# Four graph attention layers on one core: the attention weights of heads 2 and 3 of the multi-head layer transposed by the DMA crossbar in 16-bit halves

## What is computed

```python
# layer 0: scores from two weight matrices, softmax over neighbours
h1, h2, h3 = h @ W1, h @ W2, h @ W3
e = where(adj > 0, leaky_relu(h1 @ h2.T, 0.2), -1e12)
out0 = relu(softmax(e) @ h3)
# layers 1 and 3: 4 heads, scores are the sum of a row and a column term
e = where(adj > 0, leaky_relu(e_src[:, None] + e_dst[None, :], 0.2), -9e15)
out1 = elu(concat_heads(softmax(e) @ Wh))
# layer 2: multi-head attention, 4 heads of 64, biases, output projection, layernorm
s = where(adj == 0, -inf, (Q @ K.T) / 8)
out2 = layernorm(concat_heads(softmax(s) @ V) @ Wo + bo) * gamma + beta
```

## Time and profile before

| | |
|---|---|
| median of 3 runs | 2945.29 us (2944.38 to 2945.89) |
| profiled execution: span | 2943.7 us |
| around the span | not recorded apart; the median stands 1.6 us above the span |
| busy share PE / DVE / ACT / POOL | 98% / 72% / 57% / 28% |
| mean granted clock of TensorE | 0.997 of full speed |

### The profile page before, as it was taken

How to read it: one execution, slowest core, us unless ns; L and a number is a source line. 1 busy time by engine, 2 the same in 40 slices (tenths; PEclk the granted TensorE clock), 3 DMA queues, 4 the chain that set the end, 5 groups by cost and what they waited for, 6 DMA issues and landing times.

```text
span 2943.7 us, 68275 instructions
## 1 busy us (share of the span) xinstructions
PE 2887.3 (98%) x27732; PEld 2034.8 (69%) x27732; DVE 2127.5 (72%) x5596; ACT 1682.3 (57%) x3554; POOL 827.8 (28%) x917
## 2 busy tenths in 40 slices
PE   7899999999999999999999999999999999999998
PEld 5566767666767666767667767667767667776766
DVE  5576787776787776877776877776877777877764
ACT  2555655655656655656655656656656656656543
POOL 2123222323222323222233232233222233222221
PEclk9999999999999999999999999999999999999999
DMA  3001011101011101011101011101011111011010
GB/s 102 22 23 45 27 41 45 44 23 45 23 44 45 44 23 44 23 44 44 38 30 44 23 45 44 37 30 44 23 45 44 34 33 40 28 37 37 17 36 30
DMA packets 58840, 109.89 MB, mean 37 GB/s; under 512 B 5568, under 2 KB 41408, under 8 KB 58528
## 3 DMA queue, kind: packets, MB, share of 16 engines
q1 hardware_dynamic: 58032, 104.61, 10.8%
q0 software_dynamic: 496, 0.92, 0.3%
HBM read 88.21 MB, written 17.30 MB: 36 GB/s over the span
## 4 chain that ended last, share of the span: by engine, by line
PE 77%; DVE 12%; POOL 6%; issue 2%; ACT 1%; SPq 0%; DMA 0%; POOLq 0%; DVEq 0%; ACTq 0%
PE ps L972 19%; PE ps L1080 11%; PE ps L1106 8%; PE ps L1115 8%; PE ps L978 8%; PE ps L1142 8%; PE ps L1029 8%; PE ps L958 4%; DVE stats L641 3%; POOL rstd L367 3%; POOL xc L417 3%; DVE pB L753 2%; PE ps L1017 2%; DVE nb L658 1%; DVE hn L829 1%
## 5 line engine op out<-in xcount | busy, mean ns | idle before, releaser
L389 POOL TENSOR_TENSOR qx<-qx,xc 128x512 f32<-128x512 f32 x128 | 163.7, 1279 | 869.4 <-ACT qx L529 869.4
L641 DVE BATCH_NORM_STATS2 stats<-xc 128x6 f32<-128x256 f32 x384 | 134.7, 413 | 328.6 <-POOL xc L399 264.1
L448 ACT ACTIVATE hn<-xc,nb,rstd 128x256 f32<-128x256 f32 x384 | 209.1, 592 | 163.9 <-DVE nb L658 160.7
L1080 PEld LDWEIGHTS ps<-vals,pA 128*64 128x64 f32 x8192 | 253.9, 138 | 54.6 <-issue 54.5
L972 PE MATMUL ps<-wgat,hT 128*128 128x264 f32 x1024 | 267.4, 395 | 1.8 <-ACT hT L457 1.8
L1080 PE MATMUL ps<-vals,pA 128*64 128x65 f32 x8192 | 266.4, 223 | 2.1 <-DVE pA L753 2.0
L1080 PE MATMUL ps<-vals,pB 128*64 128x65 f32 x8192 | 264.0, 223 | 0.3 <-DVE pB L753 0.2
L1080 PEld LDWEIGHTS ps<-vals,pB 128*64 128x64 f32 x8192 | 249.7, 138 | 16.8 <-issue 16.7
L457 ACT COPY hT<-ps 128x1024 f32<-128x1024 f32 x128 | 129.7, 1013 | 224.0 <-PE ps L958 219.8
L1106 PE MATMUL ps<-qx,qT 64*128 64x512 f32 x1024 | 249.8, 614 | 1.1 <-DVE hn L767 0.8
L364 POOL TENSOR_SCALAR rstd<-mv 128x4 f32<-128x4 f32 x160 | 75.0, 469 | 610.2 <-DVE mv L650 610.2
(11 more groups left out here) (147 smaller groups left out, 6194.3 us busy)
## 6 DMA issues: line engine op xcount, KB each, us to landing
qT<-r_dram SPq DMA_DIRECT2D x64, 512.0 KB, 3.9
hT<-r_dram SPq DMA_DIRECT2D x64, 512.0 KB, 4.9
x_in<-in_x SPq DMA_DIRECT2D x32, 512.0 KB, 3.9
out_x<-xc SPq DMA_DIRECT2D x32, 512.0 KB, 3.0
pX<-in_adj SPq DMA_DIRECT2D x1, 1024.0 KB, 8.1
r_dram<-growT SPq DMA_DIRECT2D x64, 8.0 KB, 1.3
pX<-in_L_gnn_W SPq DMA_DIRECT2D x2, 256.0 KB, 5.2
pA<-in_L_gnn_a POOLq DMA_DIRECT2D x8, 64.0 KB, 8.8
```

Of the source, the lines that this page charges most:

```text
L641: last = nc.vector.bn_stats(stats[s][:, t, :], src[:, t, :])
L1080: last = nc.tensor.matmul(ps[lo:hi, BANK[f"G{g}.{h}"], t * DV:(t + 1) * DV], gat_p[s][h % 2][:, j, t * P + lo:t * P + hi], vals[s][:, j, h ...
```

## The change

**Transposes.** The weights of heads 0 and 1 are transposed as before. Those of heads 2 and 3 (8 of 16 tiles of a sample) no longer go through PE. Each such tile takes three steps. A split copies the 128 x 512 float32 tile, seen as 128 x 1024 16-bit words, to a buffer `halves`, with all even words first and all odd words behind them. SP issues one `dma_start_transpose`, which transposes the 128 x 1024 words in blocks of 128 and writes them back over the tile's own place in `prob2`. A join interleaves even and odd words again into `probT2`. There are three buffers `halves` (`RING` = 3), used in the order of `TURNS`; a split waits until the transpose three turns earlier has landed.

```diff
+        halves = [sb(f"halves{r}", [P, 2, N], u16) for r in range(RING)]
...
+        TURNS = (
+            (2, (2, 2, 0)), (2, (2, 3, 0)), (2, (2, 2, 1)), (2, (2, 3, 1)), (2, (2, 3, 2)),
+            (2, (2, 3, 3)), (2, (2, 2, 3)), (1, (2, 2, 2)),
+        )
...
+            def landed(self, eng, w, tile, before=0):
+                if w is None:
+                    return
+                i = self.at[w.c, tile]
+                if i // RING + 1 - before > 0:
+                    eng.wait_ge(self.sems[i % RING], 16 * (i // RING + 1 - before))
...
+        def turn(sp, w, tile):
+            sp.dma_start_transpose(words(w, tile).rearrange("p (b n) -> p b n", n=P),
+                                   turns.half(w, tile)[:, :, :].rearrange("p q n -> p (q n)")).then_inc(
+                                       turns.sem_of(w, tile), 16)
...
+            def split2(w, h, t):
+                if w is None:
+                    return
+                p2_ready[h].wait(act, w, t + 1)
+                turns.landed(act, w, (2, h, t), 1)
+                nc.scalar.copy(turns.half(w, (2, h, t))[:, :, :], pairs(w, (2, h, t))).then_inc(split_by_act.sem, 1)
...
+            def join2(w, h, t):
+                if w is None:
+                    return
+                turns.landed(dve, w, (2, h, t))
+                nc.vector.tensor_copy(joined(w, (2, h, t)), flat(w, (2, h, t))).then_inc(pT2_dve[h].sem, 1)
```

**SP's list** is now one with the other engines' and carries the transposes:

```diff
+            def slot(z, a, b, c, d, e):
+                spread(b, 1); turn2(c, 2, 0); turn2(c, 3, 0); turn2(c, 2, 1); turn2(c, 3, 1); turn2(c, 3, 2)
+                load_next(b); turn2(c, 3, 3); turn2(c, 2, 3); store(d); spread(c, 3); turn2(b, 2, 2)
```

**Order.** The slot has a sample more in its arguments (z is n+1, e is n-4) and there are 34 slots. The end of layer 3 of a sample is now done in the slot after. The first layernorm of z is taken one slot early. PE's list begins with the last transposes of heads 0 and 1, the last two `gat_aggregate` of d and `aggregate2(c, 0)`. The second pair of heads comes later than before:

```diff
-                aggregate2(c, 0)
-                gnorm[3].wait(pe, d, 4); weights_transposed2(c, 3, 0); weights_transposed2(c, 2, 2)
-                weights_transposed2(c, 2, 3); weights_transposed2(c, 3, 1); weights_transposed2(c, 3, 2)
-                pT2_act[2].wait(pe, c, 2); weights_transposed2(c, 3, 3); inverse_spread(c, 0)
-                pT2_dve[2].wait(pe, c, 2); inverse_spread(c, 1); aggregate2(c, 1); gat_aggregate(b, 1, 0)
...
+                weights_transposed2(c, 1, 1); inverse_spread(c, 0); rT_out[1].wait(pe, b)
+                weights_transposed2(c, 1, 2); gnorm[3].wait(pe, d, 2); weights_transposed2(c, 0, 2)
+                pT2_act[0].wait(pe, c, 2); weights_transposed2(c, 1, 3); weights_transposed2(c, 0, 3)
...
+                gat_aggregate(d, 3, 2)
...
+                pT2_act[1].wait(pe, c); gat_aggregate(d, 3, 3); pT2_dve[0].wait(pe, c, 2); pT2_act[1].wait(pe, c, 2)
+                aggregate2(c, 0); transposed(a, 0, 0); transposed(a, 0, 1); transposed(a, 0, 2); transposed(a, 0, 3)
+                gat_aggregate(b, 1, 0); u_columns(a, 0); u_columns(a, 1)
...
+                gnorm[1].wait(pe, b); gat_aggregate(b, 1, 1)
...
+                gat_aggregate(b, 1, 2); scores0(a, 0)
...
+                inverse_spread(c, 1)
...
+                gat_aggregate(b, 1, 3)
...
+                pT2_dve[2].wait(pe, c); pT2_act[3].wait(pe, c); aggregate2(c, 1); scores0(a, 1)
+                oT_ready.wait(pe, c, 2); scores0(a, 2); scores0(a, 3); masked0.wait(pe, a, 2); o_rows(c, 0)
+                o_rows(c, 1); o_rows(c, 2); o_rows(c, 3); masked0.wait(pe, a, 3); v_rows(a, 0, 0); v_rows(a, 0, 1)
```

DVE's list up to that point, and ACT's up to its last split:

```diff
+                gat_norm(d, 3, 1); gat_weights(d, 3, 3, 0, 1, 2); weights_out2(c, 1, 1); gat_weights(d, 3, 3, 3)
+                pT2p_ready[0].wait(dve, c, 3); weights_out2(c, 1, 2); weights_out2(c, 0, 2); weights_out2(c, 0, 3)
+                gat_norm(d, 3, 2); gat_norm(d, 3, 3); gat_weights(b, 1, 0, 0, 1, 2, 3)
+                gat_weights(b, 1, 1, 0, 1, 2, 3); gat_weights(b, 1, 2, 0); gat_norm(b, 1, 0); gat_out(d, 3, 0)
+                gat_weights(b, 1, 2, 1); inverse_sums2(c, 1); gat_weights(b, 1, 2, 2); agg2_ready.wait(dve, c)
+                join2(c, 3, 1); gat_weights(b, 1, 2, 3); gat_out(d, 3, 1); gat_norm(b, 1, 1)
+                gat_weights(b, 1, 3, 0, 1, 2, 3); join2(c, 3, 2); join2(c, 3, 0); join2(c, 2, 3); gat_norm(b, 1, 2)
...
+                weights_out2(c, 0, 1); gat_exp(b, 1); exp2(c, 2, 3); elu_relu(d, 3, 0); exp2(c, 3, 1)
+                elu_min(d, 3, 0); pT2p_ready[0].wait(act, c, 4); weights_out2(c, 1, 3); exp2(c, 3, 2)
+                elu_exp(d, 3, 0); weights_out2(c, 1, 0); split2(c, 3, 1); elu_relu(d, 3, 1); elu_min(d, 3, 1)
+                elu_m[3].wait(act, d, 2); normalised(a, 0, 0); normalised(a, 0, 1); normalised(a, 0, 2)
+                normalised(a, 0, 3); h_transposed(a, 0); exp2(c, 3, 3); inverse_out(c, 0); elu_exp(d, 3, 1)
+                split2(c, 3, 2); split2(c, 3, 3); split2(c, 2, 3); join2(c, 2, 1); xg_ready[3].wait(act, d, 2)
+                u_out(a); join2(c, 2, 0); inverse_columns(c, 1); join2(c, 2, 2); agg2_ready.wait(act, c)
```

More of the change, by code:

```diff
@@ L60, in sets @@
             return [sb(f"{name}{s}", shape) for s in range(SETS)]
-        x_in = sets("x_in", [P, NT, C])
+        x_in = [sb(f"x_in{s}", [P, NT, C]) for s in range(X_SETS)]
         xc = sets("xc", [P, NT, C])
@@ L256, in gnn_stack_kernel, with in_order @@
         x2_ready = Signal("x2_ready")
+        TURNS = (
+            (2, (2, 2, 0)), (2, (2, 3, 0)), (2, (2, 2, 1)), (2, (2, 3, 1)), (2, (2, 3, 2)),
+            (2, (2, 3, 3)), (2, (2, 2, 3)), (1, (2, 2, 2)),
+        )
+        SPLIT_BY_POOL = (
+            (2, (2, 2, 1)), (1, (2, 2, 2)), (1, (2, 2, 0)), (1, (2, 3, 0)),
+        )
+        SPLIT_BY_ACT = (
+            (2, (2, 3, 1)), (2, (2, 3, 2)), (2, (2, 3, 3)), (2, (2, 2, 3)),
+        )
+        def in_order(plan, first):
+            steps = list(first)
+            steps += [(n - stage, tile) for n in range(1, B + LAST) for stage, tile in plan
+                      if 0 <= n - stage < B]
+            return {step: i for i, step in enumerate(steps)}
@@ L284, in rows_in, with slots @@
             return ps[:, bank:bank + 2, :].rearrange("p b (t c) -> p (b t) c", c=C)
[L286 to L290, removed]
+        def slots(first, slot):
+            first(Work(0), Work(1))
+            for n in range(1, B + LAST):
+                slot(*[Work(n - d) if 0 <= n - d < B else None for d in range(-1, 5)])
         block = ctx.enter_context(nc.Block())
@@ L296, in _, with load @@
         def _(sp):
[L297 to L301, removed]
+            def load(w, ahead=X_SETS):
+                sp.dma_start(x_in[w.x][:, :, :], x_dram[w.c + ahead]).then_inc(x_loaded[w.x], 16)
             def store(w):
@@ L326, in spread, with turn2, first @@
                     sp.dma_start(dst[:, :, :], src.broadcast_to([P, 2, N])).then_inc(r_loaded[g].sem, 16)
[L328 to L331, removed]
+            def turn2(w, h, t):
+                if w is None:
+                    return
+                line = next(n for n in (split_by_act, split_by_pool) if (w.c, (2, h, t)) in n.at)
+                line.wait(sp, w, (2, h, t))
+                turn(sp, w, (2, h, t))
+            def slot(z, a, b, c, d, e):
+                spread(b, 1); turn2(c, 2, 0); turn2(c, 3, 0); turn2(c, 2, 1); turn2(c, 3, 1); turn2(c, 3, 2)
+                load_next(b); turn2(c, 3, 3); turn2(c, 2, 3); store(d); spread(c, 3); turn2(b, 2, 2)
+            def first(a, z):
+                pass
             load(Work(0), 0)
@@ L341, in _ @@
                 sp.sem_inc(x_stored[s], 16)
-                if s > 0:
+                if 0 < s < X_SETS:
                     load(Work(s), 0)
-            for n in range(B + 2):
-                slot(*[Work(n - d) if 0 <= n - d < B else None for d in range(SETS)], more=n + SETS < B)
+            slots(first, slot)
             for s in range(SETS):
@@ L621, in first @@
+                q_out(a, 1, 1); gat_row_exp(a, 1)
                 act.wait_ge(bias_in, BIASES)
                 act.wait_ge(setup_ok, SETUP)
-            slots(act, first, slot)
+            slots(first, slot)
         @block.vector
@@ L1218, in slot @@
[L1218 to L1222 removed]
+                    idle_turns(3, 5)
+                gat_aggregate(b, 1, 2); scores0(a, 0)
+                if b is None and c is not None:
+                    idle_turns(3, 32)
+                inverse_spread(c, 1)
+                if a is None and b is not None:
+                    idle_turns(3, 5)
@@ new lines, in slot @@
+                aggregate0(a, 3); qk_columns(b, "KT", 0); qk_columns(b, "QT", 1)
+                if a is None and b is not None:
+                    idle_turns(5, 10)
+                if b is None and c is not None:
+                    idle_turns(1, 76)
+                transposed(c, 3, 0); transposed(c, 3, 1); transposed(c, 3, 2); transposed(c, 3, 3)
+                qk_columns(b, "KT", 1)
+                if b is None and c is not None:
+                    idle_turns(1, 4)
+                q_rows(c, 3, 0); q_rows(c, 3, 1); qT_ready.wait(pe, b, 2); q_rows(c, 3, 2); q_rows(c, 3, 3)
@@ L1281, in first @@
                 pe.wait_ge(setup_ok, SETUP)
-            slots(pe, first, slot)
```

(1 more changed line is left out.)

344 lines of the change are left out of this document (166 added, 178 removed), and 15 rows, old and new, of the table BANK.

## The result

The changed kernel takes 2981.16 us, median of 4 runs (2973.41 to 2995.30), against 2944.84 before: 1.0126 times as long, 95% interval 1.0096 to 1.0157. It is slower by 1.3%. Faster, at 2864 us, was forecast. The four runs lie 22 us apart, and the profiled one (2973.41) is the shortest of them.

The account below looks back on a forecast made before the run. PE was taken to bound the steady slots: 30 x (3.55 won - 0.7 stall) = 85.5 us off 2943.7, plus 4 for the ends and 1.6 from span to median, gave 2864 us; range 2826 to 2950.

Parts of the forecast that it names:

- The bound and PE's gain: Steady slots: PE sets the time, and losing 32 transposes of heads 2 and 3 saves 3.55 us a slot.
- The 0.7 us of stall in the sum: Before `aggregate2(c, 1)`: PE waits for DVE's joins, offered at 25.5 us but asked at 24.9; about 0.7 us a slot.
- a sign of being wrong: Start of layer 1: the forecast is wrong if `gat_weights(b, 1, 0)` waits for `r_dram` in every slot.
- The step that failed: ACT in a steady slot: four copies out, four splits and four joins in; +5.7 us, to 58 of 85, hidden.
- the ends: First and last slots: idle turns added, transposes removed; together +4 us, between -5 and +15.
- The crossbar: SP's eight transposes a slot: 256 KB lands in about 2.6 us, step 1.3 to 2; up to 2.3 costs nothing.
- The place I feared: The seven turns before `aggregate2(c, 1)`: the kernel is slower from a crossbar step of about 2.8 us a tile.
- My rival on the slower side: Seven turns before `aggregate2(c, 1)`: at 4 us a tile, a stall of 12 us a slot, 3205 us; chance 0.17.
- Rival 1: DVE's early part: slow joins, broadcasts behind a transpose, or uncovered layer-2 chain; 2 to 3.3 us a slot; chance 0.16.
- DVE's early part: First part of a slot: DVE's tiles and joins are offered within a microsecond of when PE asks for them.
- The chain of layer 2's end: Layer 2's end: 17.9 us covered by 18.5 of PE work, charged at nothing; up to 2 us a slot if uncovered.
- the third rival: Slow crossbar step; as an extra, PE's idling may drop its clock from 2.4 to 1.2 GHz; chance 0.17.

## Why the prediction was wrong

**The bound and PE's gain: right.** 3.55 us a slot was forecast for the transposes; 3.63 came back for 3.65 of work put in again. That four buffers reach 85.84, where 85.75 was forecast, is in part luck. The 0.7 us of stall in the sum stood before `aggregate2(c, 1)`, for DVE's joins; no wait of PE for a join is in the list of four buffers. It waits about as long elsewhere, 0.7 us a slot before the first product of layer 1, for `gat_weights(b, 1, 0)`, which waits for `r_dram`. The prediction had named that very wait as a sign of being wrong.

**The step that failed** is "ACT gives up four copies ... and gets four splits and four joins ...: +5.7, to 58 of 85, hidden". I added up ACT's busy time and left out the wait that each split brings with it, `turns.landed(act, w, ..., 1)`, and so never asked what is queued behind it. ACT's busy time is indeed 58.45 in the slot. But (3,1) is three turns behind (2,0), (2,0) stands behind the broadcasts on SP, and the layernorm of a, on which PE waits next, stands behind (3,1). I had drawn up that very queue on SP, and used it only for the product at its far end, `aggregate2(c, 1)`. The place where the ring makes an engine wait was never priced. ACT waited 3.9 us a slot there and PE 2.0 for ACT; with what follows on PE, the transposes fed tile by tile and the products at the lower clock, the slot became 3.2 us longer than without the wait, where 0.7 had been allowed for all stalls. Taking the wait away alone, by a fourth buffer or by the order of ACT's list, gave 100 and 92 us back.

**The arithmetic of the miss.** Mean slot 89.0 instead of 85.75, over 29 to 30 slots: some 95 us. The rest is in the ends. From the first `scores0` product of sample 2 to that of sample 31 the four-buffer kernel needs 29 slots; what lies outside is 390.7 us, and 374.0 before. So the ends cost 17 us and not 4, the second term that was mis-sized. In the last slot with layer 2 in it PE has 39 idle turns between the two pairs of heads, about 9 us, in the kernel of four buffers, where 24 transposes took 2.7 in the same slot before. That is some 6 of the 17 us; where the rest went is open:

```profile
2810.22 7.41 PE L1065 MATMUL ps<-ident 128*128 128x128 f32 x64
2817.47 0.60 PE L1224 MATMUL ps<-ident,qx 128*128 128x128 f32 x4
2817.91 1.73 PE L1065 MATMUL ps<-ident 128*128 128x128 f32 x14
```

**The crossbar.** I took 2.6 us to landing and a step of 1.3 to 2. The shortest landing was 3.0, the median 4.3, and a turn holds SP for 1.27 (median). The place I feared, the wait for the last join, is nearly free. Of the two figures of the Trainium skill, that of "Advanced Engine Details and Errata", section "X-Bar Transpose (TRN2)", agrees with the runs in the medians, 4.3 us against 4.7 for a plain copy; the shortest were 3.0 and 2.2. That of "VectorE: DVE Perf Modes", section "The three transpose paths", taken block by block, does not hold for eight blocks in one DMA: an estimated 10.5 us by it, and none took over 8.0 with broadcasts in front. My rival on the slower side had the right sign and the right queue, SP's, but the wrong place and mechanism; its 3205 us are far off. Rival 1 had about the right size, 2 to 3.3 us of stall a slot, and none of its three causes was the one.

**DVE.** A join takes 0.75 us and not 1.1, on ACT 1.36 and not 1.01; POOL's splits are at 1.36. DVE's early part was offered within a microsecond of what PE wants, as forecast: with four buffers PE waits 0.7 us a slot for it. The chain of layer 2's end stayed covered: no wait of PE in that part stands in the list with more than a few entries.

**The clock.** Named in the third rival as an extra, not priced. It came, but in 15 of 28 slots and at an estimated 22 us of the 91. A forecast with such a gap has to count more than the gap: here the mean slot grew by 3.2 us for 2.0 us of wait.

## What to carry to other kernels

When an edit gives an engine work that begins with a wait, look at what that engine does next and for whom: price the wait at that place, not the engine's share. A ring of buffers that is filled faster than a DMA lands puts its wait into the engine that fills it, and one more buffer, or one instruction moved behind the urgent ones, is worth nearly as much here (92 to 100 us) as all the work that was saved (113 us when it was put in again). Ask of every DMA not only how long it takes but what is in front of it in its queue, and compare the order of the queue with the order in which its landings are needed.

## What the runs showed of the hardware

A crossbar transpose of 128 x 1024 16-bit words from SBUF to SBUF lands in 4.3 us (median of 256) where a plain DMA copy of the same size in its place takes 4.7. The shortest landings are 3.0 and 2.2 us, and one issue holds SP for 1.27 and 0.48 us.

A copy of 128 x 1024 16-bit words between SBUF tiles that writes them two apart takes 1.36 us on ACT and 0.75 on DVE; the split, which reads them two apart and writes them in a row, takes 1.05 on ACT and 1.36 on POOL.

Three of the four groups of DVE's `gat_weights` tiles are longer now, for instance 832 ns for those from hT to pA, 741 before; the fourth, from qT to pA, is shorter (752, 785 before). In the slot shown one took 1.47 us (at 1203.48) while POOL made three splits in a row:

```profile
1200.59 3.83 POOL L500 COPY halves<-pX 128x1024 uint16<-128x1024 uint16 x3 [8.28 <-ACT pX L644]
```

Over the whole trace, the `gat_weights` tiles during which POOL did nothing took 0.70 us each (543 of them), those with POOL's splits over more than half of their length 1.13 (94). That the two engines slow each other is argued from this coincidence; it was not tried apart.
